# Graph attention on one core: the sum over a chunk's weighted neighbours goes from VectorE to TensorE

## The chip, the core and the metric

The kernel runs as one program on one core of a Trainium2 chip. Its time is device time in microseconds (us), the median of several executions.

## What is computed

A network over 6250 nodes with 256 channels: graph attention with 8 heads of 32 channels, a mixture of experts whose router is a small attention layer, graph attention with 4 heads of 64 channels, and a second mixture of experts, all in FP32. The part that the change touches is the aggregation of the two large attention layers (lists 0 and 2). The reference of the first, cut:

```python
Wh = (x @ W.T).reshape(N, H, C)
e = e_left[src] + e_right[dst]
e = jnp.where(e >= 0, e, NEG_SLOPE * e)
e_exp = jnp.exp(e - segment_max(e, dst, num_segments=N)[dst])
denom = segment_sum(e_exp, dst, num_segments=N)
alpha = e_exp / (denom[dst] + EPS)
out = segment_sum(Wh[src] * alpha[:, :, None], dst, num_segments=N)
```

There are 200,000 directed edges (and 6250 self loops in the first layer), so each node sums about 32 rows of 256 channels, each multiplied by one weight per head.

## The kernel before, in words

The program's stages run one after the other: sorts and rankings of the edge lists, the aggregation of list 0 with the sorts of the two other lists beside it, a ranking, the small aggregation of list 1 with an expert FFN beside it, a ranking, the aggregation of list 2 with nothing beside it, and the dense layer and experts at the end. `aggregate()` (line 974) is used for list 0 (H=8, C=32, first aggregation) and list 2 (H=4, C=64, last aggregation). Both have CW = 256 channels.

**Tiles, chunks, slots, units.** The ranking sorts the nodes by degree into 49 tiles of 128, one node per partition. A tile takes `ng` slots, where a slot is one neighbour for each of the 128 nodes. All chunks of a tile have the same number of slots, at most 64; in both lists every tile has one chunk of 23 to 59 slots, 1687 in all. Eight slots are a unit (2048 FP32 values per partition).

**Gathers (POOL, L914).** GpSimd issues one indirect DMA per slot into a ring of 96 slots. Before each block of 16 slots it waits for `taken`, which VectorE raises when it has read a unit out of the ring. So POOL runs up to 96 slots ahead and is then held to VectorE's pace.

**Scores.** ScalarE copies the score columns of the chunk out of the ring (L1142 to L1146) once the last slot has landed. VectorE makes leaky ReLU, the maximum and the difference (L1055 to L1067), ScalarE takes the exponential (L1155) into PSUM (`prob`).

**The weighted sum (DVE).** `weigh` (L1042) multiplies a unit of the ring by its weights. The chunk's last unit (its tail) is written straight into `wide` in SBUF; then a loop on VectorE's own counter runs over the other units: `weigh` into `part` in PSUM, and an add of `part` to `wide` (L1080). At the chunk's end `wide` is folded from 2048 to 1024, 512 and 256 columns (L1087, L1089, L1091), `acc` is scaled by the change of the maximum (L1085) and the folded sum is added to it (L1095). At the tile's end `res` = `acc` times the inverse of the weights' sum (L1108), and ScalarE stores it.

**Order around it.** Each engine runs its own program in order; waits are on semaphores. The 49 tiles are written out one after the other (unrolled), and only chunks and units are loops. In the first aggregation VectorE does a share of the other lists' sorts after each tile's chunk (`beside.vector`), and TensorE does their transposes (`beside.tensor`); that is all that TensorE does there. In the last aggregation it does nothing.

## Time and profile before

| | us |
|---|---|
| median of 3 runs (10101.77 to 10115.83) | 10112.93 |
| span of the profiled execution | 10110.4 |
| first aggregation, 49 tiles, 1057.3 to 3676.4 | 2619.1 |
| last aggregation, 49 tiles, 6362.1 to 8751.4 | 2389.3 |
| VectorE busy in them | 2000.9 and 1432.8 |
| POOL busy in them | 1686.6 and 1701.2 |

The profiled execution has no other time than its span. The two aggregations are cut from the first score instruction of their first tile on. Busy time counts compute and gather instructions only: register, branch and semaphore instructions of an engine show up as idle time put down to "issue".

### The profile page before, as it was taken

The page shows a single profiled execution, that of the slowest core. Times are in us where ns is not written, and L with a number is a line of the kernel's source. Part 1 is how long each engine was busy: PE and PEld are TensorE (multiplying, and loading weights), DVE is VectorE, ACT ScalarE, POOL GpSimd, SP SyncE. Part 2 cuts the span into 40 slices and gives each one's busy share as a digit, 9 for nine tenths or more (in the row PEclk, how much of TensorE's full clock was granted, in tenths as well). Part 3 has the DMA queues.
Part 4 walks back from the last instruction along what each step waited for, and adds up shares of the span by engine and source line. Part 5 has one row for each costly group of instructions (what it writes and reads, how often), then busy time and mean ns, then how long its engine had stood idle before and what let it go on. Part 6 is the DMA issues. An engine that isn't in the chain of part 4 may idle for free. (4 is left out here: it accounts for less than half of the span.)

```text
span 10110.4 us, 54577 instructions
## 1 busy us (share of the span) xinstructions
PE 2288.8 (23%) x9111; PEld 1752.0 (17%) x9112; DVE 5594.3 (55%) x8828; ACT 1093.7 (11%) x2533; POOL 5337.1 (53%) x5411
## 2 busy tenths in 40 slices
PE   2112000000000002146555512000000000129995
PEld 1111000000000001135444411000000000116663
DVE  8764588788777677523333275455656556421111
ACT  1101000000000001112222201000000000002221
POOL 0025656666676654455555345776666777542221
PEclk7555555555555555578777755555555555559997
DMA  4051333433333353411111162433333333620004
GB/s 142 22 159 50 97 82 87 122 99 98 101 101 98 102 113 74 122 23 33 29 28 28 30 172 89 109 100 92 101 98 101 106 99 99 129 97 30 30 30 117
DMA packets 458121, 869.43 MB, mean 86 GB/s; under 512 B 175134, under 2 KB 294860, under 8 KB 448192
## 3 DMA queue, kind: packets, MB, share of 16 engines
q0 software_dynamic: 239536, 575.99, 23.0%
q1 hardware_dynamic: 167648, 182.04, 6.2%
q10 hardware_dynamic: 50788, 110.02, 3.3%
q14 instruction: 129, 1.06, 0.0%
q8 instruction: 20, 0.33, 0.0%
HBM read 693.35 MB, written 180.71 MB: 86 GB/s over the span
## 5 line engine op out<-in xcount | busy, mean ns | idle before, releaser
L914 POOL DMA_INDIRECT agg_ring<-table,agg_idx x4320 | 4275.8, 990 | 2329.8 <-issue 1323.4
L1042 DVE TENSOR_TENSOR agg_part<-agg_ring,agg_prob 128x2048 f32 x420 | 964.4, 2296 | 631.8 <-issue 556.2
L1080 DVE TENSOR_TENSOR agg_wide<-agg_wide,agg_part 128x2048 f32<-128x2048 f32 x420 | 960.4, 2287 | 14.4
L1786 PE MATMUL dense_tp<-all_ident,dense_xn 128*128 128x128 f32 x100 | 23.9, 425 | 2570.3 <-issue 2543.7
L1408 PE MATMUL agg_hp<-agg_xt,agg_w 128*128 128x256 f32 x1600 | 446.4, 439 | 579.4 <-ACT agg_ht L1378 340.3
L2208 DVE TENSOR_TENSOR experts_h<-experts_sg,experts_hp 128x682 f32<-128x682 f32 x106 | 91.8, 866 | 779.7 <-ACT experts_sg L2191 779.7
L2158 PE MATMUL experts_hp<-mixture_w,experts_xt 128*128 x1696 | 518.2, 458 | 0.6 <-ACT experts_xt L2187 0.6
L1408 PEld LDWEIGHTS agg_hp<-agg_xt,agg_w 128*128 128x128 f32 x1600 | 352.4, 224 | 663.8 <-ACT agg_ht L1378 360.4
L1786 PEld LDWEIGHTS dense_tp<-all_ident,dense_xn 128*128 128x128 f32 x100 | 20.3, 228 | 2571.9 <-issue 2544.5
L2129 POOL DMA_INDIRECT yc<-experts_ysb,experts_list x105 | 103.7, 987 | 685.2 <-DVE experts_ysb L2217 685.2
L1422 PE MATMUL agg_yp<-agg_w,agg_ht 128*128 128x256 f32 x1600 | 405.3, 411 | 231.0 <-remote 174.5
L1422 PEld LDWEIGHTS agg_yp<-agg_w,agg_ht 128*128 128x128 f32 x1600 | 330.4, 208 | 297.1 <-issue 246.9
L1042 DVE TENSOR_TENSOR agg_wide<-agg_ring,agg_prob 128x2048 f32 x98 | 224.2, 2288 | 275.0 <-issue 198.8
L488 POOL IOTA rank_thresholds<- 128x50 int32 x3 | 0.5, 170 | 686.4 <-POOLq L75 686.4
L2158 PEld LDWEIGHTS experts_hp<-mixture_w,experts_xt 128*128 128x128 f32 x1696 | 314.4, 190 | 174.6 <-issue 30.0
L217 PE MATMUL agg_words_turned<-all_ident,last_sort_words 128*128 128x128 f32 x48 | 10.9, 416 | 1454.1 <-issue 1454.1
L2179 PE MATMUL experts_yp<-mixture_w,experts_ht 128*128 x1260 | 309.4, 387 | 0.0
L1155 ACT ACTIVATE agg_prob<-agg_score 128x648 f32<-128x648 f32 (+1 forms) x98 | 56.7, 579 | 2332.1 <-issue 1387.9
L1055 DVE TENSOR_TENSOR agg_score<-agg_el,agg_er 128x640 f32<-128x640 f32 (+1 forms) x98 | 64.6, 659 | 410.0 <-issue 372.4
L514 POOL DMA_INDIRECT rank_start_g<-starts,rank_node_i x147 | 143.3, 975 | 225.9 <-DVE rank_degt L625 182.0
L217 PEld LDWEIGHTS agg_words_turned<-all_ident,last_sort_words 128*128 128x128 f32 x48 | 8.8, 216 | 1456.4 <-issue 1456.0
L522 POOL DMA_INDIRECT rank_wide<-copies,rank_widx x147 | 148.9, 1013 | 195.6 <-DVE rank_widx L679 154.8
(421 smaller groups left out, 6520.8 us busy)
## 6 DMA issues: line engine op xcount, KB each, us to landing
agg_ring<-table,agg_idx POOLq DMA_INDIRECT x4320
y<-agg_ysb ACTq DMA_DIRECT2D x25, 1024.0 KB
rank_y<-y SPq DMA_DIRECT2D x10, 2560.0 KB
rank_x<-x SPq DMA_DIRECT2D x30, 640.0 KB
copies<-first_sort_words SPq DMA_DIRECT2D x16, 1024.0 KB
copies<-last_sort_words ACTq DMA_DIRECT2D x16, 1024.0 KB
x<-rank_x SPq DMA_DIRECT2D x20, 640.0 KB
agg<-agg_res ACTq DMA_DIRECT2D x98, 128.0 KB
```

Of the source, the lines that this page charges most:

```text
L514: pool.indirect_dma_start(out=start_g[:, t:t + 1], out_offset=None, in_=starts.rearrange("(n a) -> n a", a=1), in_offset=bass.IndirectOffs ...
L522: pool.indirect_dma_start(out=wide[g % 2][:, u * ROW:(u + 1) * ROW], out_offset=None, in_=copies.rearrange("c (r w) -> (c r) w", w=ROW), i ...
L914: pool.indirect_dma_start(out=self.ring[:, to:to + self.RW], out_offset=None, in_=self.table, in_offset=bass.IndirectOffsetOnAxis(ap=index ...
L1042: return dve.tensor_tensor(to[:, :].rearrange("p (j h c) -> p j h c", j=UNIT, h=H), ring[:, ds(st.at(at_u), UNIT * RW)].rearrange("p (j w) ...
L1055: dve.tensor_tensor(sc3, el3, er[:, H:2 * H].unsqueeze(1).to_broadcast([P, SC // H, H]), ALU.add).then_inc(added, 1)
L1080: dve.tensor_tensor(wide[:, :], wide[:, :], part[:, :], ALU.add).then_inc(widened, 1)
L1408: mm = pe.matmul(self.hp[:, h:h + 2 * P], self.w1[:, at:at + P], xt3[:, :, k * P:(k + 1) * P], start=(k == 0), stop=(k == 1))
L1422: mm = pe.matmul(y, self.ht[:, n * 2 * P + u * P:n * 2 * P + (u + 1) * P], self.w2[:, n * D:(n + 1) * D], start=(c == 0), stop=(c == 3))
L2129: pool.indirect_dma_start(out=yc, in_=ysb[t % B][:, :], in_offset=None, out_offset=bass.IndirectOffsetOnAxis(ap=lst[:, t * 4 + 1:t * 4 + 2 ...
L2158: mm = pe.matmul(hp3[:, c, 0:HC], xt[:, kc * P:(kc + 1) * P], rhs, start=(kc == 0), stop=(kc == 1))
L2179: mm = pe.matmul(yp[:, 0:D], ht[0:m, j * P:(j + 1) * P], w2[0:m, ds(e * W2 + j * D, D)], start=(j == 0), stop=(j == HJ - 1))
L2208: dve.tensor_tensor(h[:, :].rearrange("p (c n) -> p c n", c=2), sg[:, :].rearrange("p (c n) -> p c n", c=2), hp3[:, 2:4, 0:HC], ALU.mult). ...
```

## The change

It touches `aggregate()` alone, and so the first and the last aggregation.

- `part` moves from PSUM to SBUF and becomes two buffers (`PARTS` = 2); `weigh` writes every unit, the tail too, into one of them. `wide`, `summed`, the add per unit and the three folds go.
- TensorE's `add_up` sums a unit: four matmuls with the identity as weights, each with 512 columns of `part`, all accumulated in one PSUM bank, so that 512 columns (two halves of 256) are left per chunk. Chunks use two banks in turn.
- VectorE adds the two halves of the previous chunk's bank to `acc` before the first `weigh` of a chunk; at a tile's end `res` = `acc` + half + half, and then times the inverse (three instructions where there was one).
- Before each `weigh` VectorE waits until TensorE has summed the unit before the last one (`summed`); before `res` it waits for all units of the tile.
- In the last aggregation the tiles become a loop on VectorE (`Fori(1, NT)`) and on TensorE (`Fori(0, NT)`); sizes are masked to 24 bits. ScalarE, SyncE and POOL have the instructions they had.

```diff
         assert cfg.max_slots // CH < 4096
-        wide, part, summed = s.sb("wide", [P, UC]), s.ps("part", [P, UC]), s.sb("summed", [P, CW])
...
-                def weigh(at_u, u, to):
-                    return dve.tensor_tensor(to[:, :].rearrange("p (j h c) -> p j h c", j=UNIT, h=H),
+                def weigh(at_u, u, q):
+                    return dve.tensor_tensor(part[:, ds((q % PARTS) * UC, UC)].rearrange("p (j h c) -> p j h c", j=UNIT, h=H),
...
+                        before = dve.snap(u0 + kk)
+                        last = ((kk + 1) & 1) * 512
+                        if later:
+                            dve.wait_ge(tile_done, t)
+                        dve.wait_ge(summed, before + (PARTS - 1))
+                        dve.tensor_tensor(acc[:, :], acc[:, :], sums[:, ds(last, CW)], ALU.add).then_inc(half_merged, 1)
+                        dve.wait_ge(half_merged, kk)
+                        dve.tensor_tensor(acc[:, :], acc[:, :], sums[:, ds(last + CW, CW)], ALU.add).then_inc(merged, 1)
                         dve.wait_ge(probs, kk)
                         first = u0 & 1
-                        weigh(u1, nu + first, wide).then_inc(tail, 1)
-                        n0 = dve.snap(u0 + cfg.RU)
-                        n1 = dve.snap(u1 + cfg.RU)
+                        weigh(u1, nu + first, before - 1).then_inc(tail, 1)
                         dve.wait_ge(tail, kk)
                         dve.sem_inc(st.dve_passed, 1)
-                        with dve.Fori(n0, n1) as n:
-                            u = nc.s_assert_within(n - n0, 0, CU - 2, skip_runtime_bounds_check_because="a chunk has 8 to 64 slots")
-                            dve.wait_ge(widened, n)
-                            weigh(n, u + first, part).then_inc(taken, 1)
-                            dve.wait_ge(taken, n)
-                            dve.tensor_tensor(wide[:, :], wide[:, :], part[:, :], ALU.add).then_inc(widened, 1)
+                        with dve.Fori(before, before + nu) as q:
+                            u = nc.s_assert_within(q - before, 0, CU - 2, skip_runtime_bounds_check_because="a chunk has 8 to 64 slots")
+                            dve.wait_ge(summed, q + 1)
+                            weigh(q - kk, u + first, q).then_inc(taken, 1)
                         dve.tensor_reduce(dsum[:, :], prob[:, 0:SC].rearrange("p (j h) -> p h j", h=H), AX.X, ALU.add).then_inc(totalled, 1)
                         dve.wait_ge(totalled, kk)
                         dve.tensor_tensor(den[:, :], den[:, :], prob_scale, ALU.mult).then_inc(shrunk, 1)
                         dve.wait_ge(shrunk, kk)
+                        dve.wait_ge(merged, kk)
                         dve.tensor_tensor(acc3, acc3, prob_scale.unsqueeze(2).to_broadcast([P, H, C]), ALU.mult).then_inc(scaled, 1)
-                        dve.wait_ge(widened, n1)
-                        dve.tensor_tensor(wide[:, 0:4 * CW], wide[:, 0:4 * CW], wide[:, 4 * CW:8 * CW], ALU.add).then_inc(quartered, 1)
...
-                        dve.tensor_tensor(wide[:, 0:2 * CW], wide[:, 0:2 * CW], wide[:, 2 * CW:4 * CW], ALU.add).then_inc(halved, 1)
...
-                        dve.tensor_tensor(summed[:, :], wide[:, 0:CW], wide[:, CW:2 * CW], ALU.add).then_inc(folded, 1)
+                        dve.tensor_tensor(den[:, :], den[:, :], dsum[:, :], ALU.add).then_inc(dens, 1)
                         dve.wait_ge(scaled, kk)
-                        dve.tensor_tensor(den[:, :], den[:, :], dsum[:, :], ALU.add).then_inc(dens, 1)
...
-                        dve.tensor_tensor(acc[:, :], acc[:, :], summed[:, :], ALU.add).then_inc(combined, 1)
...
+                    if later:
+                        dve.wait_ge(out_stored, t * 16)
+                    here = ((k0 + nk) & 1) * 512
+                    dve.wait_ge(summed, ((c0 + nk * ng) >> 3) + (k0 + nk) + PARTS)
+                    dve.tensor_tensor(res[:, :], acc[:, :], sums[:, ds(here, CW)], ALU.add).then_inc(half_out, 1)
+                    dve.wait_ge(half_out, t + 1)
+                    dve.tensor_tensor(res[:, :], res[:, :], sums[:, ds(here + CW, CW)], ALU.add).then_inc(all_out, 1)
+                    dve.wait_ge(all_out, t + 1)
...
+                    res3 = res[:, :].rearrange("p (h c) -> p h c", h=H)
+                    dve.tensor_tensor(res3, res3, den[:, :].unsqueeze(2).to_broadcast([P, H, C]), ALU.mult).then_inc(tile_done, 1)
+
+                tile(0, False)
+                if beside.parts:
+                    for t in range(1, NT):
+                        tile(t, True)
+                else:
+                    with dve.Fori(1, NT) as t:
+                        tile(t, True)
...
+                def add_up(q, bank, opens, closes):
+                    for i in range(UC // 512):
+                        mm = pe.matmul(sums[:, ds(bank, 512)], S["ident"][:, :], part[:, ds((q & 1) * UC + i * 512, 512)], start=opens and i == 0, stop=closes and i == UC // 512 - 1)
+                    mm.then_inc(summed, 1)
+
+                def tile(t):
+                    ng, nk, c0, k0, _ = sizes_of(pe, t)
+                    with pe.Fori(0, nk) as k:
+                        gg = c0 + k * ng
+                        kk = pe.snap(k0 + k + 1)
+                        u0, u1 = gg >> 3, (gg + ng) >> 3
+                        bank = (kk & 1) * 512
+                        n0 = pe.snap(u0 + cfg.RU)
+                        n1 = pe.snap(u1 + (cfg.RU - 1))
+                        pe.wait_ge(merged, kk)
+                        pe.wait_ge(tail, kk)
+                        add_up(u0 + kk + 1, bank, True, False)
+                        with pe.Fori(n0, n1) as n:
+                            pe.wait_ge(taken, n)
+                            add_up(n + kk, bank, False, False)
+                        pe.wait_ge(taken, n1)
+                        add_up(n1 + kk, bank, False, True)
+
+                pe.wait_ge(sized, 5)
+                pe.wait_ge(const, 6)
+                if beside.parts:
+                    for t in range(NT):
+                        tile(t)
+                        beside.tensor(pe, t)
+                else:
+                    with pe.Fori(0, NT) as t:
+                        tile(t)
```

On VectorE, the unit loop and the chunk's end of a tile of the first aggregation stood so before (ISA, REGISTER_ALU and branch rows are the sequencer's; a wait on a semaphore stands at the row it holds):

```order
L1042 ISA [waits agg0_widened]
L1042 ISA
L1042 TENSOR_TENSOR agg_part<-agg_ring,agg_prob 128x2048
L1080 TENSOR_TENSOR agg_wide<-agg_wide,agg_part 128x2048 [waits agg0_taken]
L1075 ISA
L1075 COMPARE_AND_BRANCH
L1081 TENSOR_REDUCE agg_dsum<-agg_prob 128x8
L1083 TENSOR_TENSOR agg_den<-agg_den,agg_prob 128x8 [waits agg0_totalled]
L1085 TENSOR_TENSOR agg_acc<-agg_acc,agg_prob 128x256 [waits agg0_shrunk]
L1086 REGISTER_ALU
L1087 TENSOR_TENSOR agg_wide<-agg_wide 128x1024 [waits agg0_widened]
L1089 TENSOR_TENSOR agg_wide<-agg_wide 128x512 [waits agg0_quartered]
```

The same place in the changed kernel:

```order
L1047 ISA [waits agg0_summed]
L1047 ISA
L1047 REGISTER_ALU
L1047 TENSOR_TENSOR agg_part<-agg_ring,agg_prob 128x2048
L1086 ISA
L1086 COMPARE_AND_BRANCH
L1090 TENSOR_REDUCE agg_dsum<-agg_prob 128x8
L1092 TENSOR_TENSOR agg_den<-agg_den,agg_prob 128x8 [waits agg0_totalled]
L1095 TENSOR_TENSOR agg_acc<-agg_acc,agg_prob 128x256 [waits agg0_merged,agg0_shrunk]
L1096 TENSOR_TENSOR agg_den<-agg_den,agg_dsum 128x8
```

The 2048-column add and the folds are gone; a unit has one compute row and five rows of the sequencer (four before), and its wait is on TensorE's `summed`.

On VectorE, the rows between the last score instruction and the loop, before:

```order
L1042 ISA [waits agg0_probs]
L1042 ISA
L1042 REGISTER_ALU
L1042 ISA
L1042 TENSOR_TENSOR agg_wide<-agg_ring,agg_prob 128x2048
L1075 ISA [waits agg0_tail]
```

And now:

```order
L1078 REGISTER_ALU [waits agg0_summed]
L1078 REGISTER_ALU
L1078 ISA
L1078 TENSOR_TENSOR agg_acc<-agg_acc,agg_sums 128x256
L1080 ISA [waits agg0_half_merged]
L1080 TENSOR_TENSOR agg_acc<-agg_acc,agg_sums 128x256
L1047 ISA [waits agg0_probs]
L1047 REGISTER_ALU
L1047 ISA x2
L1047 TENSOR_TENSOR agg_part<-agg_ring,agg_prob 128x2048
L1086 UNCONDITIONAL_BRANCH [waits agg0_tail]
```

Two 256-column adds from PSUM stand ahead of the tail's `weigh`, behind a wait for `summed`, with address rows between them. In all a tile of the last aggregation has 12 sequencer rows and 4 per unit on VectorE before, and 33 and 5 per unit in the looped code.

On TensorE, where a tile of the first aggregation had only the sort's transposes and one of the last had nothing, there now stands, for each unit of the loop:

```order
L1131 REGISTER_ALU [waits agg0_taken]
L1131 REGISTER_ALU
L1131 ISA
L1131 MATMUL agg_sums<-agg_part,all_ident 128x512
L1131 ISA
L1131 MATMUL agg_sums<-agg_part,all_ident 128x512
L1131 ISA
L1131 MATMUL agg_sums<-agg_part,all_ident 128x512
L1131 ISA
L1131 MATMUL agg_sums<-agg_part,all_ident 128x512
L1146 ISA
L1146 COMPARE_AND_BRANCH
```

The four matmuls of a unit have eight sequencer rows with them. The first and the last unit of a chunk stand outside this loop with the same four matmuls.

## Rows read from the trace of the kernel before

**Rows 1.** the page, part 1: busy us, share of the span, instructions

```profile
PE 2288.8 (23%) x9111; PEld 1752.0 (17%) x9112; DVE 5594.3 (55%) x8828; ACT 1093.7 (11%) x2533; POOL 5337.1 (53%) x5411
```

**Rows 2.** aggregations, windows: PE, PEld, DVE, ACT, POOL busy us (x), granted clock, DMA share, GB/s

```profile
1057.30:3676.40 2619.10, 49.97 (x208) 39.87 (x208) 2000.87 (x2128) 175.60 (x450) 1686.57 (x1692) 0.50 0.37 96
6362.10:8751.40 2389.30, 0.00 (x0) 0.00 (x0) 1432.84 (x1400) 111.01 (x398) 1701.21 (x1693) 0.50 0.39 99
```

**Rows 3.** first aggregation, lines by form: count, busy us, mean ns, idle before

```profile
L914 POOL DMA_INDIRECT agg_ring<-table,agg_idx x1692 | 1686.7, 997 | 905.4 <-issue 520.7 <-DVE agg_part L1042 384.7
L1042 DVE TENSOR_TENSOR agg_part<-agg_ring,agg_prob 128x2048 f32 x210 | 482.3, 2296 | 140.4 <-issue 75.4 <-DVE agg_wide L1080 50.1 <-DVE agg_wide L1042 14.9
L1080 DVE TENSOR_TENSOR agg_wide<-agg_wide,agg_part 128x2048 f32<-128x2048 f32 x210 | 480.2, 2287 | 7.2
...
L1042 DVE TENSOR_TENSOR agg_wide<-agg_ring,agg_prob 128x2048 f32 x49 | 112.1, 2288 | 120.4 <-ACT agg_prob L1155 61.5 <-issue 58.9
...
L1087 DVE TENSOR_TENSOR agg_wide<-agg_wide 128x1024 f32<-128x1024 f32 x49 | 59.9, 1222 | 0.0
...
L1089 DVE TENSOR_TENSOR agg_wide<-agg_wide 128x512 f32<-128x512 f32 x49 | 33.9, 692 | 1.7
L1108 DVE TENSOR_TENSOR agg_res<-agg_acc,agg_den 128x256 f32<-128x256 f32 x49 | 21.5, 439 | 14.7 <-DVE agg_den L1104 6.0 <-remote 3.8 <-issue 3.6
L1095 DVE TENSOR_TENSOR agg_acc<-agg_acc,agg_summed 128x256 f32<-128x256 f32 x49 | 20.8, 425 | 0.0
L1091 DVE TENSOR_TENSOR agg_summed<-agg_wide 128x256 f32<-128x256 f32 x49 | 20.8, 425 | 1.7
```

**Rows 4.** last aggregation, lines by form

```profile
L914 POOL DMA_INDIRECT agg_ring<-table,agg_idx x1693 | 1702.1, 1005 | 671.1 <-issue 524.9 <-DVE agg_part L1042 146.2
L1042 DVE TENSOR_TENSOR agg_part<-agg_ring,agg_prob 128x2048 f32 x210 | 482.2, 2296 | 491.5 <-issue 480.9 <-DVE agg_wide L1080 5.4 <-DVE agg_wide L1042 5.2
...
L1142 ACT ACTIVATE agg_el<-agg_ring x153 | 39.2, 256 | 333.4 <-issue 333.4
...
L1055 DVE TENSOR_TENSOR agg_score<-agg_el,agg_er 128x320 f32<-128x320 f32 x49 | 24.1, 492 | 293.1 <-issue 283.1 <-ACT agg_el L1146 6.5 <-DMA agg<-agg_res 3.5
```

**Rows 5.** DVE's timeline, first aggregation: start, duration, idle before

```profile
1308.99 2.30 DVE L1042 TENSOR_TENSOR agg_part<-agg_ring,agg_prob 128x2048 f32 x1 [0.74 <-issue]
...
1314.04 2.30 DVE L1042 TENSOR_TENSOR agg_part<-agg_ring,agg_prob 128x2048 f32 x1 [0.44 <-DVE agg_wide L1080]
```

**Rows 6.** DVE's timeline, one tile of the last aggregation

```profile
7005.73 0.49 DVE L1055 TENSOR_TENSOR agg_score<-agg_el,agg_er 128x320 f32<-128x320 f32 x1 [4.30 <-issue]
...
7019.08 2.29 DVE L1042 TENSOR_TENSOR agg_part<-agg_ring,agg_prob 128x2048 f32 x1 [4.74 <-issue]
...
7026.08 2.29 DVE L1042 TENSOR_TENSOR agg_part<-agg_ring,agg_prob 128x2048 f32 x1 [2.38 <-issue]
...
7053.39 0.49 DVE L1055 TENSOR_TENSOR agg_score<-agg_el,agg_er 128x320 f32<-128x320 f32 x1 [4.23 <-issue]
```

**Rows 7.** POOL's timeline in that tile

```profile
7021.18 0.95 POOL L914 DMA_INDIRECT agg_ring<-table,agg_idx  x1 [0.30 <-issue]
7029.16 0.94 POOL L914 DMA_INDIRECT agg_ring<-table,agg_idx  x1 [7.03 <-DVE agg_part L1042]
7030.41 0.95 POOL L914 DMA_INDIRECT agg_ring<-table,agg_idx  x1 [0.30 <-issue]
```

**Rows 8.** FFN beside the middle aggregation, windows: columns as in rows 2

```profile
4500.00:5000.00 500.00, 312.29 (x1201) 256.31 (x1200) 183.39 (x507) 128.47 (x243) 262.80 (x278) 0.80 0.17 32
4605.00:4610.00 5.00, 3.24 (x8) 2.52 (x8) 0.00 (x0) 0.84 (x2) 1.81 (x2) 0.50 0.11 7
4615.00:4620.00 5.00, 5.00 (x25) 4.41 (x24) 4.53 (x10) 0.92 (x2) 3.78 (x5) 1.00 0.10 10
```

**Rows 9.** PE's timeline there

```profile
4606.76 3.78 PE L1408 MATMUL agg_hp<-agg_xt,agg_w 128*128 128x256 f32 x8 [6.57 <-issue]
...
4617.68 3.62 PE L1408 MATMUL agg_hp<-agg_xt,agg_w 128*128 128x256 f32 x16
```

35 lines of the change are left out of this document (15 added, 20 removed).

## The prediction

> **What bounds the kernel now.** The page first: VectorE (5594 us) and POOL (5337 us) are each busy for about half of the 10110.4 us, so neither bounds the whole [rows 1], and the change touches only two stages. So I cut those out. The first aggregation takes 2619.1 us with VectorE 2000.9 busy and POOL 1686.6, the last 2389.3 us with 1432.8 and 1701.2 [rows 2]. They hold the same 259 products and nearly the same 1692 gathers. The first also holds the sorts' work on VectorE.
>
> Next the groups by form, and in them the idle time. In the first aggregation POOL waits 384.7 us for VectorE's weigh; VectorE's weigh in turn waits little (140.4) [rows 3]. So VectorE holds POOL there: 2619.1 / 49 = 53.5 us a tile, and a unit takes 5.05 us, two instructions of 2.3 us and small gaps [rows 5]. In the last aggregation it is otherwise: POOL waits for VectorE only 146.2 us, VectorE is busy 60% of the time, and its weigh stands behind 491.5 us of idle time of which 480.9 are "issue", its score 283.1, ScalarE's copy 333.4 [rows 4]. A unit there starts 7.0 us after the last one with the same two instructions of 2.3 us [rows 6]. That idle time sits where the order has register, semaphore and branch rows. One tile took 47.66 us from score to score [rows 6], and the order counts 12 sequencer rows and 4 per unit on VectorE, 28 for the four loop units of that tile: 1.70 us for each.
>
> What slows them? The stage's work on POOL is the same in both aggregations: gathers follow each other at 1.25 us where nothing holds them [rows 7], and even there POOL has 7 us waits. All in, a gather costs 2389.3 / 1693 = 1.41 us in the last aggregation. My reading: there the machine is held by something that gathers load and that the sequencers of VectorE and ScalarE share; when it is full the sequencers step slowly, units are released late, and POOL is braked until the load fits. In the first aggregation VectorE's own work brakes POOL, so the load is rarely full (unit pitch 5.05). This is inferred, not shown: "issue" names no releaser.
>
> **The change, part by part.**
>
> VectorE's compute. Gone in each aggregation: 210 adds of 2.287 us, 480 us, and folds and final add, 59.9 + 33.9 + 20.8 + 20.8 = 135 us [rows 3]. Added: two merges and two adds into res per tile. No row adds from PSUM at 256 columns; between the 256-column add in SBUF (0.425) and twice that I take 0.43, since weigh costs 2.296 into PSUM and 2.288 into SBUF [rows 3]: 49 x 4 x 0.43 = 84 us. Net -531 us, -10.8 us a tile. Products to SBUF: nothing, by the same two rows.
>
> What that is worth. First aggregation: VectorE falls to 2001 - 531 = 1470 us, 30 us a tile, and stops being what holds POOL. What holds it next is the last aggregation's limit, 2389 us for the same gathers, plus the sorts' rows. Last aggregation: VectorE already has spare time, so 531 us less of it is worth nothing. Its cover is the 7 us unit pitch; if the sequencers' pace were no limit, POOL's waits of 146.2 us would be what could be had.
>
> TensorE. 259 units x 4 matmuls of 512 columns in FP32. The profile has FP32 matmuls of 256 columns, each call leaving two records (at L1408 the code issues 32 calls a block for 25 blocks, and 1600 records stand in the trace): 16 records in 3.62 us at granted clock 1.00, 8 in 3.78 at 0.50 [rows 8, 9], so 0.226 and 0.47 per 256 columns. A unit is 8 records of 512 columns: 3.6 us at 2.4 GHz, 7.6 at 1.2 GHz. Per tile 5.3 units: 19 or 40 us, against the 48.8 of a tile; TensorE fits at either level, and a unit's 7.6 us is below the 10 us in which POOL fills eight slots (8 x 1.25). The clock stands at 0.50 in both aggregations now [rows 2]; in the FFN it rose to 1.00 within the matmuls that followed a 6.57 us pause [rows 8, 9]. With waits for units between the bursts I expect mixed levels. The Trainium skill (TensorE: Matmul & The Clock Gate, HAM oscillation) says that TensorE falls back when it waits between bursts of work; by it the 7.6 us stands throughout, which the sum above bears without a cost.
>
> New waits. weigh of unit q waits for TensorE's sum of q-2: at 7.6 us a unit VectorE's burst over a tile is 40 us instead of 5 x 5.05. Behind the last weigh, res waits for one or two sums, 4 to 15 us. The tile after it needs its slots landed and scored; POOL's 96 slots of lead (2.8 tiles of 34.4) hide that while the total stays under the tile's time: 40 + 2.3 (first weigh) + about 4 for scores and exponential = 46, just under 48.8. Costed at nothing; without that cover see the cold rival.
>
> Rows. Per unit TensorE gets 16 records (8 matmul, 8 weight load) and 8 sequencer rows, VectorE one more sequencer row and one compute row less; per tile TensorE about 12 and VectorE about 20 sequencer rows. 259 x 24 + 49 x 32 = 7,800 rows more in each aggregation. If what is shared is loaded by each instruction and not by gathers alone, they cost. Lower bound 0. Upper bound from the FFN stretch, where 500 us hold 278 gathers and 3151 other rows: (500 - 278 x 1.41) / 3151 = 0.034 us a row [rows 8]. That stretch isn't full all the time, so I take 0.02: 156 us per aggregation. The Trainium skill (NOTIFIC — the notification-queue block, Overflow: three behaviours, one of which stalls the engine) describes a path that carries every engine's event records and can push back on the engines when its internal queues fill. It gives no price for a row, and no run here shows that this is the path; by it the term has the sign that I give it.
>
> **Sum.** First aggregation: 2389 + (208 + 208 + 728 + 52 = 1196 more visible rows of the sorts [rows 2]) x 0.02 = 24, + 156 = 2569, against 2619: -50. Last: +156. Together +106 on 10110.4, 10216; the profile's span lies 2.5 below the median, so 10220. At price 0 it is -230 and 0: 9880. At 0.034: 2389 + 41 + 265 = 2695, +76, and +265: 10450.
>
> **The rivals.**
>
> Gathers alone load it (0.18). Rows cost nothing; the first aggregation loses its brake: 9880. For it: POOL waits 384.7 us for VectorE there. Against: nothing that separates gathers from rows.
>
> The slow stepping goes away (0.13), because VectorE's unrolled code was what slowed it: then both stages run at POOL's floor, 1.25 to 1.31 a gather, about 2215: -404 and -174, 9530. In the first aggregation the same unrolled code runs fast, which speaks against it [rows 5]. The Trainium skill (Runtime: NRT & Kernel Launch, Instruction fetch mechanics) says the other way round that branches break sequential prefetch; by it the loop is the one that pays.
>
> The slow stepping stays and more rows meet it (0.19). VectorE's looped tile has 33 + 5 per unit = 53 sequencer rows for 28; at 1.70 us each that is 90 us a tile. It brakes POOL and so relieves itself, so not in full; a third of the excess is 49 x (90 - 47.7) / 3 = +690 in the last aggregation alone, about 10,900. It decides once slow steps remain in over half of the tile's rows.
>
> TensorE stays at 1.2 GHz and its chain decides (0.08): 46 us plus the wait before res, up to 15, is 61 a tile, +12 x 49 = +600 in the last aggregation, less if sums overlap: 10,300 to 10,700.
>
> **How the numbers follow.** The forecast holds 0.42; its own range is 9880 to 10450. A difference within 0.2% (20 us) is about what a measurement of this kernel can't tell from none. Faster: the first two rivals, 0.31, and 0.06 of the forecast at row prices under 0.012. Slower: the last two, 0.27, and 0.30 of the forecast. The same: 0.06. The range leaves out the floor case and the upper half of the slow stepping: 9750 to 10750.
>
> **What would show it.** Right: last aggregation longer than 2389 with TensorE busy 900 to 1900 us, weigh behind "issue" still; first aggregation at 2500 to 2620 with the unit pitch up from 5.05 and POOL's wait for weigh well below 384.7. Wrong: a first aggregation near 2400 (rows are free) or near 2220 (no slow stepping), weigh waiting mainly for agg_sums (TensorE's chain), or a last aggregation beyond 2700.

## The result, and the profile after

The changed kernel takes 10568.95 us (median of 4, 10508.55 to 10577.39) against 10114.38 for the kernel before: 1.0443 times as long, 95% interval 1.041 to 1.0476. Two more comparisons gave 1.0475 (1.0449 to 1.0501) and 1.0444 (1.0395 to 1.0493). The forecast was 10220, so the direction is right and the loss about four times as large as forecast.

The page's part 1 of the changed kernel (busy us, share, instructions), beside [rows 1]:

```profile
PE 4439.2 (42%) x13255; PEld 2616.5 (25%) x13256; DVE 4527.0 (43%) x8410; ACT 1089.6 (10%) x2533; POOL 5219.0 (49%) x5411
```

VectorE lost 1067 us of work and TensorE gained 2150, and the kernel got slower. Both aggregations, windows with the columns of [rows 2]:

```profile
1052.20:3911.10 2858.90, 1125.53 (x2280) 469.99 (x2280) 1464.44 (x1918) 173.87 (x450) 1659.53 (x1691) 0.69 0.34 88
6626.90:9219.80 2592.90, 1080.73 (x2072) 435.92 (x2072) 901.17 (x1190) 107.80 (x398) 1605.16 (x1691) 0.71 0.36 91
```

The first took 2619.1 us and now takes 2858.9 (+240), the last 2389.3 and now 2592.9 (+204). These are 443 of the 465 us between the two profiled spans. In the two repeats of the changed kernel the first took 2821.1 and 2847.1 and the last 2608.5 and 2610.4 us: one trace of an aggregation is good to some 20 us in the last and 40 us in the first. TensorE's granted clock averages 0.69 and 0.71 where it stood at 0.50, so it runs at both of its levels, 1.2 and 2.4 GHz. A matmul record of 512 columns takes 0.68 us on average, but records overlap; TensorE is busy for 4.2 us a unit (1080.73 / 259).

The groups of the last aggregation by form (count, busy us, mean ns, idle before and its releasers), beside [rows 4]:

```profile
L914 POOL DMA_INDIRECT agg_ring<-table,agg_idx x1691 | 1605.8, 950 | 970.7 <-issue 510.3 <-DVE agg_part L1047 460.4
L1131 PE MATMUL agg_sums<-agg_part,all_ident 128*128 x2072 | 1080.7, 682 | 1634.9 <-DVE agg_part L1047 1120.1 <-issue 514.9
L1047 DVE TENSOR_TENSOR agg_part<-agg_ring,agg_prob x259 | 590.5, 2287 | 812.1 <-issue 522.4 <-PE agg_sums L1131 195.4 <-remote 84.2
...
L1111 DVE TENSOR_TENSOR agg_res<-agg_acc,agg_sums 128x256 f32<-128x256 f32 x49 | 20.6, 421 | 590.6 <-remote 421.8 <-issue 145.8 <-PE agg_sums L1131 23.0
```

POOL now waits 460.4 us for weigh instead of 146.2. VectorE waits 590.6 us before `res`, of which 421.8 are "remote": TensorE's sums are what it waits for, but the semaphore rose at a time at which the trace finds no instruction that ended. The same groups in the first aggregation, beside [rows 3]:

```profile
L914 POOL DMA_INDIRECT agg_ring<-table,agg_idx x1691 | 1659.5, 981 | 1177.3 <-DVE agg_part L1047 661.9 <-issue 515.4
L1131 PE MATMUL agg_sums<-agg_part,all_ident 128*128 x2072 | 1087.7, 687 | 1630.0 <-DVE agg_part L1047 1111.1 <-issue 518.8
L1047 DVE TENSOR_TENSOR agg_part<-agg_ring,agg_prob x259 | 591.8, 2287 | 790.0 <-issue 314.9 <-PE agg_sums L1131 245.9 <-remote 178.3
...
L1111 DVE TENSOR_TENSOR agg_res<-agg_acc,agg_sums 128x256 f32<-128x256 f32 x49 | 20.6, 421 | 188.1 <-remote 162.5 <-issue 25.6
```

Here POOL's wait for weigh went up from 384.7 to 661.9 us, though the adds that were to be its cause are gone. Idle time before weigh went from 140.4 to 790.0 us: 245.9 for TensorE's sums and 178.3 "remote" are new, and "issue" went from 75.4 to 314.9.

For all runs but the paced ones the last aggregation is, within 20 us (28 in the kernel before with half the gathers), the sum of three things in POOL's rows: gathers, issue gaps, and the wait for weigh. In the changed kernel 1605.8 + 510.3 + 460.4 = 2576.5 of 2592.9. The first two are POOL's floor, some 2110 to 2145 us where the products don't lengthen a gather. In the one trace of the kernel before a gather took 1005 ns and the two came to 2227 us; so against that trace gathers and gaps gave back 111 us and the wait for weigh took 314 more. Why gathers took 1005 ns there and 947 to 965 in all other last aggregations whose products don't lengthen them is not known. So the question is why `weigh` comes late. One tile shows it, VectorE's timeline (start, duration, idle before):

```profile
7900.62 2.29 DVE L1047 TENSOR_TENSOR agg_part<-agg_ring,agg_prob  x1 [4.07 <-issue]
7912.40 2.29 DVE L1047 TENSOR_TENSOR agg_part<-agg_ring,agg_prob  x1 [9.49 <-remote]
7934.78 2.29 DVE L1047 TENSOR_TENSOR agg_part<-agg_ring,agg_prob  x1 [20.10 <-remote]
...
7943.74 0.42 DVE L1111 TENSOR_TENSOR agg_res<-agg_acc,agg_sums 128x256 f32<-128x256 f32 x1 [4.68 <-PE agg_sums L1131]
```

And TensorE's in the same stretch:

```profile
7903.30 5.14 PE L1131 MATMUL agg_sums<-agg_part,all_ident 128*128 x8 [2.71 <-issue]
7915.03 6.09 PE L1131 MATMUL agg_sums<-agg_part,all_ident 128*128 x8 [6.59 <-DVE agg_part L1047]
7937.41 5.15 PE L1131 MATMUL agg_sums<-agg_part,all_ident 128*128 x8 [16.29 <-DVE agg_part L1047]
```

A weigh needs the sum of the unit before the last one. For the weigh at 7934.78 that is the sum which starts at 7903.30 and is recorded as done at 7908.44, 26.3 us earlier; VectorE itself was free from 7914.68 on, and sat idle for 20.10 us. The weigh at 7912.40 comes 11.8 us after the end of its sum (7900.59).

The same matching, made for every wait before `res` in the last aggregation, splits its 590.6 us: TensorE's last sum of the tile was still running for 113 us, and 477 us lie behind its recorded end, over 10 us in 17 of the 49 tiles and up to 34 us. Before weigh, the waits over 0.6 us add up to 807 us, 144 with the sum still running and 662 with the sum done and VectorE free; in the first aggregation 771, 191 and 580. The 662 and 580 also hold the time of VectorE's own register and branch rows.

### The profile page after: what moved, and what is told of

It reads as the page before. It is cut to its first block and busy times, and to the rows that moved or that the text cites. A ratio compares the mean times of both kernels' runs of the same rounds, so it can differ in the third digit from the quotient of the medians.

```text
span 10575.3 us, 71454 instructions
## 1 busy us (share of the span) xinstructions
PE 4439.2 (42%) x13255; PEld 2616.5 (25%) x13256; DVE 4527.0 (43%) x8410; ACT 1089.6 (10%) x2533; POOL 5219.0 (49%) x5411
## 5 line engine op out<-in xcount | busy, mean ns | idle before, releaser
L914 POOL DMA_INDIRECT agg_ring<-table,agg_idx x4320 | 4156.7, 962 | 2932.5 <-issue 1309.2
L1131 PE MATMUL agg_sums<-agg_part,all_ident 128*128 x4144 | 2168.4, 685 | 3265.0 <-DVE agg_part L1047 2231.2
L1131 PEld LDWEIGHTS agg_sums<-agg_part,all_ident 128*128 128x128 f32 x4144 | 876.0, 221 | 4548.7 <-issue 4548.4
L1047 DVE TENSOR_TENSOR agg_part<-agg_ring,agg_prob x518 | 1182.3, 2287 | 1602.1 <-issue 837.3
L1451 PEld LDWEIGHTS agg_hp<-agg_xt,agg_w 128*128 128x128 f32 x1600 | 351.0, 222 | 534.7 <-ACT agg_ht L1421 271.0
L1111 DVE TENSOR_TENSOR agg_res<-agg_acc,agg_sums 128x256 f32<-128x256 f32 x98 | 41.3, 421 | 778.8 <-remote 584.3
L1829 PE MATMUL rank_tp<-all_ident,rank_xn 128*128 128x128 f32 x300 | 75.0, 421 | 444.2 <-issue 218.2
L1844 PE MATMUL rank_mp<-rank_wcat,rank_xt 128*128 128x272 f32 (+2 forms) x600 | 191.0, 485 | 153.7 <-issue 80.1
L190 DVE TENSOR_TENSOR last_sort_words<-last_sort_words 128x1024 f32<-128x1024 f32 x176 | 209.2, 1230 | 94.2 <-ACT last_sort_words L236 74.8
L2222 PEld LDWEIGHTS experts_yp<-mixture_w,experts_ht 128*128 128x128 f32 x1260 | 230.0, 189 | 77.3 <-issue 34.8
L1421 ACT ACTIVATE agg_ht<-agg_hp,agg_b 128x256 f32<-128x256 f32 x400 | 163.0, 473 | 813.2 <-remote 538.2
```

The costliest lines, as they stand in the source:

```text
L190: dve.tensor_tensor(b[:, :, half, :], a[:, :, 0, :], a[:, :, 1, :], op).then_inc(self.cmp_done, 1)
L914: pool.indirect_dma_start(out=self.ring[:, to:to + self.RW], out_offset=None, in_=self.table, in_offset=bass.IndirectOffsetOnAxis(ap=index ...
L1047: return dve.tensor_tensor(part[:, ds((q % PARTS) * UC, UC)].rearrange("p (j h c) -> p j h c", j=UNIT, h=H), ring[:, ds(st.at(at_u), UNIT ...
L1131: mm = pe.matmul(sums[:, ds(bank, 512)], S["ident"][:, :], part[:, ds((q & 1) * UC + i * 512, 512)], start=opens and i == 0, stop=closes a ...
L1421: last = act.activation(self.ht[:, n * 2 * P:(n + 1) * 2 * P], self.hp[:, h:h + 2 * P], ACT.Gelu, bias=self.b1[:, n:n + 1])
L1451: mm = pe.matmul(self.hp[:, h:h + 2 * P], self.w1[:, at:at + P], xt3[:, :, k * P:(k + 1) * P], start=(k == 0), stop=(k == 1))
```

## The experiments

The runs stand in five groups, each with the kernel before timed beside it. In the first, third, fourth and fifth group it took 10090, 10088, 10125 and 10096 us; these are called the usual conditions. In the second group it took 9114.79: the quick conditions, kept apart here, which turned out to be the most telling. Times of an aggregation come from one trace each, and the kernel before has such a trace only from before these groups.

**The masks alone.** Sizes are masked to 24 bits, as in the changed kernel; all later versions of the kernel before have this too. It corrects the section on the change: ScalarE does get some eight more register rows a tile, and VectorE five.

```diff
-            return nc.s_assert_within(ng, 1, CH, ...), nk, c0, k0, missing
+            return nc.s_assert_within(ng & MASK24, 1, CH, ...), nk & MASK24, c0 & MASK24, k0 & MASK24, missing & MASK24
```

> The kernel before with the changed kernel's masks on the tile sizes and nothing else of the change: some 8 more register rows a tile on VectorE and on ScalarE in both large aggregations. Shared-load theory (every instruction row costs about 0.02 to 0.03 us while the aggregation is full): +15 to +25 us in the last aggregation, little in the first. Sequencer-step theory (1.4 to 1.7 us for each row on VectorE's path): 49 x 8 x 1.5 = up to +590 us in the last. Handshake theory (the loss is VectorE and TensorE waiting for each other): 0.

1.0073 (1.0048 to 1.0098). The first aggregation takes 2623.9 us (+5), the last, in windows:

```profile
6383.80:8811.60 2427.80, 0.00 (x0) 0.00 (x0) 1430.43 (x1400) 109.58 (x398) 1623.44 (x1691) 0.50 0.38 97
```

+38 us against the trace of the kernel before: more than the shared load asks, far less than a price of 1.5 us for each row. It is little above what separates two traces of one kernel.

**Products in SBUF, and idle matmuls beside them.** `part` goes to SBUF and VectorE still adds; then TensorE gets the changed kernel's matmuls, on a constant tile and into a spare bank.

```diff
-        wide, part, summed = s.sb("wide", [P, UC]), s.ps("part", [P, UC]), ...
+        wide, part, summed = s.sb("wide", [P, UC]), s.sb("part", [P, UC]), ...
```
```diff
+                def add_up():
+                    for i in range(UC // 512):
+                        pe.matmul(spare[:, 0:512], S["ident"][:, :], still[:, :], start=i == 0, stop=i == UC // 512 - 1)
...
+                        pe.wait_ge(tail, kk)
+                        add_up()
+                        with pe.Fori(n0, n1) as n:
+                            pe.wait_ge(taken, n)
+                            add_up()
```

> As masks, and the product buffer in SBUF instead of PSUM, VectorE still adds. All theories: the same as masks, within 20 us; if writing or reading the products in SBUF costs something beside the gathers (two SBUF inputs of the 2048-column add), then the add gets longer than 2.29 us and both aggregations grow.

> As sbuf_part, and TensorE runs the changed kernel's four 512-column matmuls for each unit, paced by the same semaphores, on a constant tile into a spare bank; nobody waits for it, VectorE still adds. Shared-load theory: the last aggregation grows by about 150 to 200 us and the first by less, though no engine waits for TensorE. Handshake theory: no change against sbuf_part in either aggregation.

1.0126 (1.0087 to 1.0165) and 1.0194 (1.0166 to 1.0222). The last aggregation takes 2485.4 and 2481.0 us: the idle matmuls cost nothing there; the first takes 54 us more with them (2584.4 and 2638.8). In the lines by form of the last aggregation with products in SBUF a gather is longer:

```profile
L914 POOL DMA_INDIRECT agg_ring<-table,agg_idx x1691 | 1940.5, 1148 | 535.6 <-issue 516.7 <-DVE agg_part L1043 18.9
L1081 DVE TENSOR_TENSOR agg_wide<-agg_wide,agg_part 128x2048 f32<-128x2048 f32 x210 | 481.7, 2294 | 7.3
```

A gather takes 1148 ns on average where it took 960 with the masks alone (1623.44 / 1691), and VectorE's add with both inputs in SBUF keeps its 2294: the gather is what gives way. The Trainium skill (SBUF — State Buffer, Who interferes with whom) says that a VectorE instruction with two SBUF inputs contends with a GpSimd instruction that reads SBUF. The trace agrees, at some 320 us over 1691 gathers. The changed kernel has no such add, so this is no part of its loss, and the run prices TensorE's rows under other conditions than the changed kernel's.

The run shows one thing more. With gathers this far apart VectorE's "issue" before weigh in the burst is 68.4 us where the masks alone have 332.5, POOL waits for weigh 18.9 us where it waited 271.1, and yet the aggregation is no shorter: it lies on POOL's floor, which is now 1940.5 + 516.7 = 2457 us.

**The tile loop undone.** In the changed kernel's last aggregation the tiles are written out on both engines (`if True:` for `if beside.parts:`).

> The changed kernel with the last aggregation's tiles written out again as in the first. Shared-load theory: some 20 fewer rows a tile, 1000 rows, -20 to -30 us in the last aggregation. If branches of the looped code cost fetches: -100 us or more. If the loop saved something: slower than the changed kernel.

1.0498 (1.0466 to 1.0531); last aggregation 2598.7 against 2592.9. The loop is worth nothing either way.

**The second group, quick conditions.** Idle matmuls in the last aggregation, products in PSUM, nobody waits; every second gather left out of the changed kernel (`step` is 2 from the second ring on, and the sums then read stale rows); four product buffers; and `res` made behind the next tile's scores (`finish` makes the `res` of the tile before).

```diff
-                for j in range(SLOTS):
+                for j in range(0, SLOTS, step):
```
```diff
-PARTS = 2
+PARTS = 4
```
```diff
+                        if later:
+                            dve.wait_ge(merged, kk)
+                            finish(t - 1, later > 1)
                         dve.wait_ge(probs, kk)
                         first = u0 & 1
```

> The kernel before with the masks, products in PSUM, and in the last aggregation alone four idle 512-column matmuls a unit on TensorE, for which nobody waits. The last run of this kind had the products in SBUF, where the two-input add lengthened gathers and VectorE's sequencer was no longer slow, so it could not price a row in the slow state. Shared-load theory: last aggregation 2428 (masks) plus 5300 rows x 0.02 to 0.03 = 2530 to 2590. Handshake theory: 2428.

> The changed kernel with every second gather left out from the second ring on (the sums then read rows gathered earlier, so the output differs): POOL's floor halves to about 1060 us an aggregation. Handshake theory: the chain of scores, weigh, TensorE's sums and res holds the pace by itself, some 38 to 48 us a tile, last aggregation 1900 to 2400, first 2500 to 2800. Gather-load theory: the slow sequencer steps and late releases vanish, and the last aggregation falls below 1800.

> The changed kernel with four product buffers instead of two: weigh waits for the sum of the unit four before. Handshake theory: VectorE's waits for TensorE inside the burst go (246 and 195 us), but TensorE's 4.3 us a unit stays on the chain before res: 0 to -100 us an aggregation. Shared-load theory: no change.

> The changed kernel with a tile's res made behind the next tile's scores, from acc after its merge (written for one chunk a tile, as here), so that VectorE does not stand still for TensorE's last sums. Handshake theory: the wait before res (188 us in the first, 591 in the last aggregation) goes or shrinks by most: last aggregation -200 to -400, first -100 to -200. Shared-load theory: no change, the time comes back as slow steps.

Against 9114.79 for the kernel before: idle matmuls 1.0023 (1.0013 to 1.0033), half the gathers 0.8784 (0.8769 to 0.8798), four buffers 0.9793 (0.9777 to 0.9809), late `res` 0.9853 (0.9836 to 0.9869). Windows of both aggregations with idle matmuls, where VectorE works as before:

```profile
1028.20:3447.40 2419.20, 50.24 (x208) 40.19 (x208) 2000.93 (x2128) 172.52 (x450) 1700.96 (x1692) 0.50 0.40 104
5624.20:7789.60 2165.40, 1038.12 (x2072) 422.57 (x2072) 1433.62 (x1400) 105.68 (x398) 1628.17 (x1693) 0.76 0.43 109
```

The same kernel takes 2640 and 2463 us under the usual conditions (below), 2419 and 2165 here. VectorE's timeline and POOL's waits in the last aggregation:

```profile
6630.74 2.30 DVE L1045 TENSOR_TENSOR agg_part<-agg_ring,agg_prob 128x2048 f32 x1 [0.44 <-DVE agg_wide L1083]
...
6635.80 2.30 DVE L1045 TENSOR_TENSOR agg_part<-agg_ring,agg_prob 128x2048 f32 x1 [0.44 <-DVE agg_wide L1083]
```

```profile
POOL agg_ring L914 <- issue: 514.1, 1688, 0.3
POOL agg_ring L914 <- DVE agg_part L1045: 6.0, 5, 4.8
```

A unit follows in 5.06 us where [rows 6] have 7.0, and POOL waits 6.0 us where the same kernel waits 311.3 under the usual conditions: VectorE's idle time called "issue" is gone though nothing in the code is. Here the last aggregation lies on POOL's floor, 1628 + 514 us, and a quicker VectorE can bring nothing there. Four product buffers:

```profile
1030.00:3248.70 2218.70, 1040.74 (x2280) 460.37 (x2280) 1455.56 (x1918) 171.22 (x450) 1679.77 (x1692) 0.73 0.44 114
5434.40:7576.00 2141.60, 1009.54 (x2072) 430.85 (x2072) 895.72 (x1190) 105.69 (x399) 1612.78 (x1693) 0.73 0.43 110
```

2218.7 and 2141.6: both on or near the floor. VectorE's wait before `res` in the last aggregation:

```profile
DVE agg_res L1111 <- PE agg_sums L1131: 427.5, 49, 9.1
```

All 49 waits have TensorE's last matmul as releaser, and `res` starts 0.24 us behind its end: hand-overs are prompt here with all gathers running. With half the gathers, windows and VectorE's waits of the last aggregation:

```profile
1030.40:3113.50 2083.10, 1054.91 (x2280) 448.30 (x2280) 1462.67 (x1918) 172.20 (x450) 871.98 (x876) 0.75 0.25 67
5099.10:6665.50 1566.40, 1004.61 (x2072) 413.32 (x2072) 900.11 (x1190) 105.72 (x398) 834.67 (x877) 0.83 0.31 80
```

```profile
DVE agg_part L1052 <- PE agg_sums L1136: 328.1, 161, 4.8
DVE agg_res L1116 <- PE agg_sums L1136: 112.1, 49, 2.3
```

This is the changed kernel's chain alone: 2083.1 / 49 = 42.5 us a tile in the first and 1566.4 / 49 = 32.0 in the last aggregation. These waits for TensorE have its last matmul as releaser, at 2.0 us each inside the burst (the loop over a chunk's units) and 2.3 before `res`.

**Back under the usual conditions.** The changed kernel again, the kernel before with half the gathers, four buffers again, and four buffers with late `res`.

> The changed kernel once more, beside the kernel before on the same chip, because the last call ran on a chip on which the kernel before took 9115 instead of 10090 to 10114 us and no sequencer step was slow. Theory that slow sequencer steps make the loss: on a chip without them both aggregations run near POOL's floor of about 2150 to 2250 us and the change is 1.5 to 2.5% faster than before (first aggregation 2419 before); on a chip with them again 4 to 5% slower. Handshake theory: slower on either chip.

> The kernel before with the masks and with every second gather left out (output differs). It gives VectorE's chain without POOL's floor. If no step is slow: first aggregation about 2250 to 2400 (VectorE at 46 to 49 us a tile), last 1650 to 1800 (34 to 37 a tile); the changed kernel gave 2083 and 1566 so. If steps are slow also at half the gathers, they don't come from gathers.

> Four product buffers, again, beside the changed kernel on the same chip. Without slow steps: as before, 2.1% faster than the kernel before, and faster than the changed kernel by 0 to 1%. With slow steps: the buffers take the waits inside the burst, 100 to 300 us better than the changed kernel, still at or above the kernel before.

> Four product buffers and the late res together. Without slow steps: both aggregations at POOL's floor, 2190 and 2145, 8900 or 2.3% faster than before, no better than four buffers alone by more than 30 us. With slow steps: the chain a tile is shortest here, so the best of the changed family: 150 to 400 us better than the changed kernel.

The changed kernel gives 1.0475, the kernel before with half the gathers 0.8685 (0.8662 to 0.8708), four buffers 1.0671 (1.061 to 1.0731), four buffers and late `res` 1.0523 (1.0497 to 1.0549). The kernel before with half the gathers, windows:

```profile
1052.70:3445.70 2393.00, 50.28 (x208) 40.13 (x208) 1995.69 (x2128) 173.32 (x450) 860.94 (x876) 0.50 0.22 58
5638.20:7397.30 1759.10, 0.00 (x0) 0.00 (x0) 1431.16 (x1400) 105.94 (x398) 835.17 (x876) 0.50 0.28 72
```

48.8 and 35.9 us a tile. VectorE's timeline in the last aggregation:

```profile
6606.47 2.30 DVE L1048 TENSOR_TENSOR agg_part<-agg_ring,agg_prob 128x2048 f32 x1 [0.44 <-DVE agg_wide L1086]
...
6611.53 2.30 DVE L1048 TENSOR_TENSOR agg_part<-agg_ring,agg_prob 128x2048 f32 x1 [0.44 <-DVE agg_wide L1086]
```

The unit pitch is 5.06 us, as under the quick conditions. So fewer gathers remove the slow stepping under the conditions that have it. The changed kernel's chain without slow steps is shorter than this one by 6.3 and 3.9 us a tile; it was measured under the quick conditions only, so no run shows whether half the gathers also make its hand-overs prompt under the usual ones. Four buffers, 2% faster under the quick conditions, are the slowest version here. VectorE's and POOL's waits in its last aggregation (2761.3 us):

```profile
DVE agg_res L1111 <- remote: 961.8, 34, 55.6
DVE agg_part L1047 <- issue: 346.7, 110, 6.8
```

```profile
POOL agg_ring L914 <- DVE agg_part L1047: 639.0, 47, 32.4
```

The buffers let VectorE run ahead in the burst, and the time came back as 961.8 us of "remote" before `res`. Matched with TensorE's records, all of VectorE's idle time before `res` is 1249 us: 314 with the last sum still running and 935 behind its recorded end. The same kernel under the quick conditions has 416 and 12. This pair of runs is the clearest evidence that hand-overs from TensorE come late under the usual conditions, and that the conditions and not the kernel make them so.

**TensorE's rows, its length, and the spacing of gathers.** Idle matmuls once more; products and identity in BF16, one pass a matmul and less precise sums; one small POOL memset after each gather, in the changed kernel and in the kernel before.

```diff
+                    pool.memset(self.pace[:, at_p:at_p + 1], 0.0).then_inc(self.paced, 1)
```

> Products in PSUM, idle matmuls in the last aggregation, nobody waits for them. On a chip with slow steps: shared-load theory (each row 0.02 to 0.03 us) 2530 to 2590 in the last aggregation against 2428 with masks alone; if TensorE's rows cost nothing, 2420 to 2440. On a chip without them 2165 as before.

> The changed kernel with the products rounded to BF16 and a BF16 identity, so that a matmul is one pass (half of TensorE's records and about a quarter of its time; the sums lose precision). With slow steps: shared-load theory 2072 rows fewer, -40 to -60 us an aggregation; handshake theory: TensorE's 4.3 us a unit becomes 1, so -100 to -300 us; gather theory: little, since a quicker chain only lets gathers come closer. Without slow steps: both at POOL's floor, 2150 to 2200.

> The changed kernel with one small POOL memset after each gather of the large aggregations, so that a gather takes 1.30 to 1.45 us instead of 1.25. Gather theory, on a chip with slow steps: most slow steps go, and an aggregation takes 1692 times the new pitch: at 1.40 us 2370, which is 200 us less than the changed kernel in the last aggregation and 400 less in the first, and the whole is faster than the kernel before. Shared-load by rows and handshake theories: no gain or slower. On a chip without slow steps: 1692 x the added pitch slower than the changed kernel.

> The kernel before with the masks and the same memset. Gather theory, with slow steps: last aggregation at 1692 times the pitch, 2300 to 2400, slow steps gone; first unchanged at 2600 or below, since VectorE's 49 us a tile bound it. Otherwise: slower by up to 1692 x 0.1 to 0.2 us in the last.

Idle matmuls 1.0227 (1.021 to 1.0244), last aggregation:

```profile
6419.40:8882.90 2463.50, 1162.23 (x1724) 402.99 (x1725) 1430.96 (x1400) 109.60 (x398) 1624.95 (x1692) 0.60 0.38 96
```

2463.5 us, 36 above the masks alone, for over 4400 rows more: 0.008 us a row. But the window holds only 1724 of TensorE's 2072 records, and the whole run lost 2.3%, not the 0.7% of the masks. TensorE's timeline shows why:

```profile
7438.18 1.01 PE L1121 MATMUL agg_spare<-agg_still,all_ident 128*128 128x512 f32 x1 [1.79 <-issue]
...
8836.24 196.46 PE L1121 MATMUL agg_spare<-agg_still,all_ident 128*128 128x512 f32 x451 [1.10 <-issue]
9062.42 2.37 PE L1811 MATMUL dense_tp<-all_ident,dense_xn 128*128 128x128 f32 x10 [29.72 <-issue]
```

In such stretches TensorE's records stand about 2.8 us apart and a unit's eight take some 21 us, where a unit without slow steps takes 3.6. TensorE fell behind VectorE by up to 470 us, finished 150 us after the aggregation (9032.7), and held up the dense layer, whose first record comes 179.5 us behind the aggregation instead of 31.2. So TensorE is stepped slowly too when it runs by itself beside dense gathers, and 0.008 us a row is the price to the others while it is braked, not the whole price. In the changed kernel no unit took TensorE longer than 6.8 us.

BF16 1.0367 (1.0339 to 1.0395), windows:

```profile
1056.90:3763.80 2706.90, 541.66 (x1224) 165.64 (x1244) 1466.66 (x1918) 175.84 (x450) 1667.42 (x1691) 0.51 0.36 93
6462.40:9110.20 2647.80, 475.44 (x987) 127.65 (x1036) 902.32 (x1190) 108.69 (x398) 1608.02 (x1692) 0.51 0.35 89
```

Half of TensorE's time is gone; the first aggregation gains 150 us on the changed kernel's 2858.9 (114 on the 2821.1 of a repeat) and the last loses 55 (37 against 2610.4). Paced changed kernel 1.0414 (1.0383 to 1.0445), last aggregation 2589.6: no gain. Paced kernel before 0.9992 (0.9982 to 1.0003), lines by form of its last aggregation:

```profile
L920 POOL DMA_INDIRECT agg_ring<-table,agg_idx x1692 | 1633.6, 965 | 557.7 <-issue 500.0 <-DMA rank_x<-x 36.2 <-DVE agg_part L1052 11.5
L1052 DVE TENSOR_TENSOR agg_part<-agg_ring,agg_prob 128x2048 f32 x210 | 482.3, 2297 | 108.1 <-issue 51.2 <-DVE agg_wide L1090 35.9 <-DVE agg_wide L1052 20.9
...
L924 POOL MEMSET agg_pace<- 128x1 f32 x1692 | 196.3, 116 | 30.6 <-issue 29.2
```

VectorE's idle time before weigh fell from 491.5 to 108.1 us and POOL's wait for it from 146.2 to 11.5, yet the aggregation takes 2429.0 us, as with the masks alone. POOL's timeline shows where it went:

```profile
7006.37 0.95 POOL L920 DMA_INDIRECT agg_ring<-table,agg_idx  x1 [0.19 <-issue]
7007.31 0.12 POOL L924 MEMSET agg_pace<- 128x1 f32 x1
7007.62 0.95 POOL L920 DMA_INDIRECT agg_ring<-table,agg_idx  x1 [0.19 <-issue]
...
7010.49 0.95 POOL L920 DMA_INDIRECT agg_ring<-table,agg_idx  x1 [0.37 <-issue]
```

The memset (0.12 us) fits into the 0.30 us gap and leaves the pitch at 1.25 us; but now POOL's own gaps grow, from 0.19 to 0.37 us in these lines (mean pitch of gathers less than 2 us apart: 1.30), and 177 gathers come over 2 us after the one before, most of them 2.1 or 2.8 us. The brake moved from VectorE to POOL and the total stayed (2429.0 against the masks' 2427.8). So this wasn't the test of a slower pitch that it was meant to be; it suggests that the last aggregation's 2430 us don't depend on which engine is stepped slowly. The first aggregation took 2564.7 us, 59 less than with the masks alone, which nothing here explains.

**The wait alone.** Idle matmuls as before, and VectorE waits for TensorE as in the changed kernel, but gives up no work; beside it the changed kernel a third time.

```diff
+                            dve.wait_ge(made_up, (n - (cfg.RU - 1)) + kk)
                             weigh(n, u + first, part).then_inc(taken, 1)
```

> The kernel before with the masks, in the last aggregation the idle matmuls on a constant tile, and before each weigh VectorE waits until TensorE is through with the unit before the last one, as in the changed kernel. VectorE still makes its adds. With slow steps: if the wait on TensorE is what costs, the last aggregation goes from 2464 to 2550 to 2700 with releases that come well after TensorE's last matmul; if it is not, 2460 to 2480. Without slow steps: 2165, POOL's floor.

> The changed kernel as a control. On a chip with slow steps 2590 to 2610 in the last and 2820 to 2860 in the first aggregation, 1.042 to 1.050 of before. On one without: 2150 to 2165 and 2200 to 2300, 0.975 to 0.985 of before.

1.0148 (1.0131 to 1.0166) and 1.0444. The last aggregation takes 2513.4 us, 50 more than without the wait. (The whole run is quicker than the one without it, since TensorE, which VectorE now waits for, has all its 2072 records inside the aggregation and doesn't hold up the dense layer.) VectorE's waits in it, and POOL's:

```profile
DVE agg_part L1047 <- remote: 534.7, 44, 17.8
DVE agg_part L1047 <- issue: 196.1, 80, 17.1
```

```profile
POOL agg_ring L914 <- issue: 514.3, 1640, 6.0
POOL agg_ring L914 <- DVE agg_part L1047: 352.6, 51, 20.7
```

VectorE waits 534.7 us in 44 places for something "remote", up to 17.8 us: the late release is there as soon as VectorE waits for TensorE at all. Its idle time before the weighs of the burst goes from 389 to 812 us, while the aggregation grows by 50: most of it was room.

## Why the prediction was wrong in size

**The reading of the last aggregation** held: VectorE had spare time, less work on it was worth nothing, and what held the pace was tied to the gathers. With half of them it goes (35.9 us a tile), with a small POOL instruction beside each it moves from VectorE to POOL at the same total, and under the quick conditions it isn't there at all. That it isn't a property of the kernel but of conditions around it I had not thought of. The price of a step was misread: the tile of [rows 6] has 34 sequencer rows on VectorE in the trace, five in each loop unit, not 28, and they start 1.40 us apart (5 x 1.40 is the unit pitch of 7.0), not 1.70.

**The row term** was mis-sized and stands for the wrong thing. Forecast: 7,800 rows at 0.02 us, 156 us an aggregation. The count was near (71454 rows against 54577 in the two pages, 8440 more an aggregation). Measured in the last aggregation: 0.008 us a row of TensorE, 36 us, and 38 us for the masks. BF16, with half of TensorE's records, was no shorter in the last aggregation. The Trainium skill (NOTIFIC — the notification-queue block, Overflow: three behaviours, one of which stalls the engine) says that the block's internal pipeline pushes back rather than lose a record; the sign agrees with the 36 us, and no run here shows that this is the path. The same page (Constraints, capacities, measured rates) puts the cost of emitting a record at zero cycles of the engine, which the prediction's "no price for a row" passes over; rows had a price here, and the measurement decides.

The last aggregation's +204 is 38 (masks) + 36 (idle TensorE) + 50 (the wait for it) + 80 for what remains: `res` behind TensorE's last sums, the merges, and whatever else the real sums bring. These are differences of single traces from different groups, each little above the 20 us between two traces of one kernel, and TensorE was braked in one of them and not in the other; the order of the parts holds, the split does not. The forecast of +156 was near this +204 by luck, since it stood for rows.

**"Costed at nothing", the new waits,** is the step that failed. I set the chain against the tile's 48.8 us with TensorE at its slow level and found room. TensorE was quicker than that (4.2 us a unit, not 7.6), and the chain without interference is 32.0 us. But under the usual conditions a hand-over from TensorE to VectorE can come 10 to 34 us late (477 of the 591 us before `res`), and the chain grew to 2592.9 / 49 = 52.9 us, beyond POOL's 43. A wait across engines has the price that its release has in that stretch, and I priced TensorE's work.

**"Stops being what holds POOL"** failed with it, in the first aggregation: forecast -50, measured +240, which is 290 of the 349 us between forecast and measurement. VectorE's work did fall to 1464 us, as forecast (1470). But a tile there is a chain: scores, burst, the sorts' share, `res`. With half the gathers it is 42.5 us against 48.8 before; with all of them it came to 58.3 and POOL waited 661.9 us. Less busy time on VectorE wasn't less chain. What the trace shows of the growth is weigh's idle time, 140.4 to 790.0 us; no experiment under the usual conditions takes the waits alone in this aggregation, so its share between late hand-overs and slow steps is read from the rows, not tested.

**The rivals.** The slow stepping meeting more rows was nearest in mechanism (0.19), but at +690 in one aggregation too dear, since it brakes POOL and so itself; with its +690 the sum is 10,800, not the 10,900 given. TensorE held at 1.2 GHz: the clock averaged 0.7. The case without slow stepping (9530) is what the quick conditions show for the machine, where the kernel before itself took 9115, and not what the change does.

**What stays open.** What makes the sequencers slow and the releases late when gathers run densely, and why one group in five was free of it. Every execution timed here has its span and clock recorded, so no run can tell whether the recording has a part in it. The changed kernel itself was not run under the quick conditions; two of its variants gained 1.5 and 2.1% there, and its chain (42.5 and 32.0 us a tile) lies under POOL's floor (2219 / 49 = 45.3 and 43.7), so it would likely be faster than the kernel before there. That is argued, not shown. No version tried beats the kernel before under the usual conditions.

## What to carry to other kernels

Before moving work off an engine, ask what the stage's floor is (here POOL's gathers and gaps) and which chain feeds it; take the chain's length with its waits, not an engine's busy time. A hand-over inside the innermost step has to be priced by how late releases come in that very stretch, and idle time called "issue" on several engines at once was the warning here. And an engine for which nobody waits is not free: idle matmuls fell behind and held up the next stage. When the same kernel's time can differ by 10% from one group of runs to the next, compare only with the kernel before of the same group, and try a variant under both conditions: four buffers were 2% faster in one and 6.7% slower in the other.

## What the runs showed of the hardware

- The kernel before took 10088 to 10125 us in four groups of runs and 9115 in one, on a chip (3) that gave 10096 in another group. In stretches of dense gathers VectorE's register and branch rows start 1.40 us apart under the usual conditions: a unit pitch of 7.0 us against 5.06 under the quick ones.
- In the kernel before, half the gathers took VectorE's slow stepping away; one POOL memset a gather moved it from VectorE to POOL, and the aggregation kept its 2429 us.
- TensorE steps slowly as well: records of idle matmuls beside the gathers stood 2.8 us apart in such stretches, and TensorE fell up to 470 us behind VectorE.
- In the tile shown VectorE's weigh started 26.3 us after the recorded end of the sum it waited for. Before `res` such delays add up to 477 us in the changed kernel and 935 us with four buffers, and to 12 us with four buffers under the quick conditions.
- VectorE's add with both inputs in SBUF lengthened gathers from 960 to 1148 ns on average and kept its own time.
